# Loading the input tiles of a delta-rule attention kernel batch by batch

## The reference

```
x = x + layernorm(attention(layernorm(x)))
x = x + layernorm(ffn(layernorm(x)))
```

```
pred = wk @ S;  err = (v - pred) * beta;  S = S + outer(wk, err);  o = (rk @ S) * gate
```

## Time and profile before

| | us |
|---|---|
| median of 3 runs | 2324.56 |
| lowest, highest | 2321.91, 2326.44 |
| span of the profiled execution | 2313.7 |
| PE, DVE, ACT, POOL busy in it | 2084.1, 1992.1, 1774.0, 1729.0 |

### The profile page before, as it was taken

How to read it: one execution, slowest core, us unless ns; L and a number is a source line. 1 busy time by engine, 2 the same in 40 slices (tenths; PEclk the granted TensorE clock), 3 DMA queues, 4 the chain that set the end, 5 groups by cost and what they waited for, 6 DMA issues and landing times. The chain is left out here.

```text
span 2313.7 us, 123730 instructions
## 1 busy us (share of the span) xinstructions
PE 2084.1 (90%) x50216; PEld 1316.0 (57%) x50216; DVE 1992.1 (86%) x5810; ACT 1774.0 (77%) x3756; POOL 1729.0 (75%) x3099
## 2 busy tenths in 40 slices
PE   1679999999999999999999999999999987499997
PEld 1346666666666666666655656566666654255554
DVE  5388999999999999999889999899999994588886
ACT  3667888888888888888877878788888744477775
POOL 2668888888888888888888888888888854244443
PEclk7789999999999999999999999999999988799999
DMA  2122333333333333333333333333333222488885
GB/s 86 48 65 80 98 100 98 98 98 95 99 97 99 94 94 95 95 94 94 93 91 93 94 96 91 94 97 96 100 96 99 82 78 67 150 225 229 225 231 129
DMA packets 156632, 247.69 MB, mean 107 GB/s; under 512 B 39544, under 2 KB 39552, under 8 KB 156064
## 3 DMA queue, kind: packets, MB, share of 16 engines
q1 hardware_dynamic: 156064, 239.78, 36.6%
HBM read 104.40 MB, written 67.11 MB: 74 GB/s over the span
## 5 line engine op out<-in xcount | busy, mean ns | idle before, releaser
L800 DVE TENSOR_TENSOR ps_elim<-ps_elim,sys 128x30 f32<-128x30 f32 (+14 forms) x1920 | 543.3, 326 | 0.7
L808 DVE TENSOR_TENSOR sys<-sys,ps_elim 128x30 f32<-128x30 f32 (+14 forms) x1920 | 534.6, 316 | 1.0
L925 PE MATMUL ps_v<-wv,xt 128*128 128x512 f16 x1536 | 435.2, 389 | 39.6 <-DVE rhs L831 16.5
L925 PE MATMUL ps_y<-wo,ot 128*128 128x512 f16 x1536 | 406.1, 386 | 17.3 <-DVE x L852 9.5
L962 PEld LDWEIGHTS ps_chain<-rhs,t_t 32*32 32x32 f32 x16384 | 257.3, 144 | 110.6 <-issue 110.5
L962 PE MATMUL ps_chain<-rhs,t_t 32*32 32x32 f32 x16384 | 286.1, 218 | 13.9 <-issue 8.5
L709 ACT ACTIVATE state<-ps_s 128x512 f32<-128x512 f32 x128 | 76.5, 598 | 265.6 <-PE ps_s L1024 263.6
L1024 PEld LDWEIGHTS ps_s<-err,key_b 32*32 32x32 f32 x16384 | 172.1, 106 | 147.4 <-issue 147.2
L1310 PE MATMUL ps_f<-wq,f_xq 128*128 128x512 f16 x1024 | 242.5, 381 | 6.8 <-DVE f_xq L1276 6.8
L538 POOL TENSOR_TENSOR x_part<-x_hat,x_part 128x512 f16<-128x512 f32 x128 | 148.7, 1162 | 131.6 <-ACT x_hat L645 111.5
L1024 PE MATMUL ps_s<-err,key_b 32*32 32x32 f32 x16384 | 205.5, 195 | 34.2 <-issue 34.2
(11 more groups left out here) (163 smaller groups left out, 5123.6 us busy)
## 6 DMA issues: line engine op xcount, KB each, us to landing
x_in<-in_L_attn_x SPq DMA_DIRECT2D x128, 256.0 KB
kbd<-kt SPq DMA_DIRECT2D x512, 64.0 KB, 2.1
key_bd<-key_t SPq DMA_DIRECT2D x512, 64.0 KB, 2.4
x_res<-in_L_attn_x SPq DMA_DIRECT2D x128, 256.0 KB
x_scratch<-x SPq DMA_DIRECT2D x128, 256.0 KB, 6.3
f_x<-x_scratch SPq DMA_DIRECT2D x32, 1024.0 KB, 7.6
out<-f_res SPq DMA_DIRECT2D x128, 256.0 KB, 3.9
gate<-gates SPq DMA_DIRECT2D x128, 7.9 KB
```

Of the source, the lines that this page charges most:

```text
L800: dve.tensor_tensor(tmp, factors(r, c, first, end)[:, c - first:C - 1 - first, c - first:c - first + 1].to_broadcast(shape), sys[:, r, c:c ...
L808: dve.tensor_tensor(dst, dst, tmp, ALU.add).then_inc(elim_done[r], 1)
L925: last = pe.matmul(out, lhs[:, a, kb, :], weights[:, w, kb, :], start=(i == 0), stop=(i == 3 * KB - 1))
```

## The change

Each of the two loads is issued as four transfers, one per batch, of 32 rows of 2 KB each, in a loop. All four add to the same semaphore, so the waits count 64 per tile and not 16. Buffers, lags, order and all other work stay.

```diff
-                    sp.dma_start(tile(x_in, l % 4), rows(io["x"], base, j, LAG_LOAD)).then_inc(x_loaded[l % 4], 16)
+                    for b in range(B):
+                        sp.dma_start(x_in[C * b:C * b + C, l % 4, :], io["x"][b, C * n:C * n + C, :]).then_inc(x_loaded[l % 4], 16)
...
-                    sp.dma_start(tile(x_res, l % 2), rows(io["x"], base, j, LAG_Y)).then_inc(res_loaded[l % 2], 16)
+                    for b in range(B):
+                        sp.dma_start(x_res[C * b:C * b + C, l % 2, :], io["x"][b, C * n:C * n + C, :]).then_inc(res_loaded[l % 2], 16)
...
-                    act.wait_ge(x_loaded[l % 4], quads(base, j, LAG_STATS) * 16 + 16)
+                    act.wait_ge(x_loaded[l % 4], quads(base, j, LAG_STATS) * (16 * B) + 16 * B)
...
-                    act.wait_ge(x_loaded[l % 4], quads(base, j, LAG_XHAT) * 16 + 16)
+                    act.wait_ge(x_loaded[l % 4], quads(base, j, LAG_XHAT) * (16 * B) + 16 * B)
...
-                    dve.wait_ge(res_loaded[l % 2], halves(base, j, LAG_RES) * 16 + 16)
+                    dve.wait_ge(res_loaded[l % 2], halves(base, j, LAG_RES) * (16 * B) + 16 * B)
```

## The result

The changed kernel takes 2289.72 us (4 runs, 2287.3 to 2295.06) against 2325.5 us of the kernel before on the same chip: a ratio of 0.985 (95% interval 0.983 to 0.988), faster by 36 us. The forecast was faster by 11 us, 2313.5 us. The profile is of the slowest of the four runs (2295.06). One run in all that follows, the first of a repeat of the changed kernel, was in a slower state of the chip (granted clock 0.833 against 0.97, 2381.62 us) and is left out of its median.

The account below looks back on a forecast made before the run. SP's late issuing, beside the PE and DVE pair, was taken as the bound; with SP at 13.5 us a step, -6 - 3 - 1 - 4 + 3 = -11 us gave span 2302.7, plus 10.9 made 2313.5 us; full range 2297 to 2352.

Parts of the forecast that it names:

- What bounds the kernel: Attention part: PE and DVE tied as a pair, with SP, issuing all transfers, a bound beside them in two long stretches.
- Issues added: SP, each step: six more load issues at 0.48 us plus 0.04 gap, +3.12 us; the two that stay, -0.26.
- The jam: SP, at the four `key_bd` behind loads and gates: spread loads take off 4.1 us a step, leaving 0.6 for the gates.
- Collisions: SP's groups of issues: 0.9 more clashes a step with instruction queue packets at 0.77 us each, +0.7 us.
- Waits that go: Whole kernel: DVE's waits for `x_res` -6 us, PE's for `key_bd` -3 and for `kbd` -1.
- The start: Filling of the kernel: the first tiles' loads land sooner, so the third tile's statistics start earlier, -4 us.
- Costs elsewhere: PE's "issue" waits before `ps_s`: spread loads share engines with instruction fetch, +3 us, bounds 0 and 17.
- What lies around the span: Outside the profiled span: the runs' median lay 10.9 us above it, carried over unchanged to the forecast time.
- SP's relief is worth more: Rival, attention steps: 0.15 us per step comes back over 91 steps, 14 us more, 2299 us; chance 0.10.
- SP gets fuller: Rival: SP's step grows to 14.7 us, +55 us where SP is the bound, 2375; decided at 0.59 us pitch; chance 0.25.
- Quarters do not spread: Rival: 32-partition transfers run at a quarter rate, jam stays, some 113 steps grow about 2.9 us, 2650; chance 0.03.

Follow-up runs that it names:

- second profile: The kernel before, unchanged, profiled once more: 2324.01 us for a span of 2322.3.
- start-only kernel: Kernel before with only the `x_in` loads of the first four tiles split into four transfers: 2319.22 us, ratio 0.9985.
- only `x_in`: Kernel before with `x_in` split into four transfers and `x_res` left as one: 2301.43 us, ratio 0.990; repeated, 2300.86 us, ratio 0.989.
- gates in two parts: Kernel before with the gate transfer of 127 partitions cut into one of 112 and one of 15, loads single: 2302.65 us, ratio 0.990.
- the eighths: Changed kernel with both loads in eight transfers of 16 rows instead of four of 32: 2622.3 us, ratio 1.128 of the kernel before.

## Why the prediction was right in kind and wrong in size

*What bounds the kernel.* Right. SP was late in the long stretches, the jam made it so, and the edits that remove the jam, two of them without touching a load, gain 19 to 24 us.

*Issues added.* 0.48 us taken, 0.421 (`x_in`) and 0.425 (`x_res`) measured in the median, 0.310 at the least (the changed kernel's issues by line, ns min/median/max):

```profile
L431 SPq DMA_DIRECT2D x_in<-in_L_attn_x x512: 310/421/2059, 38.2 to 1757.4; - x171
...
L463 SPq DMA_DIRECT2D x_res<-in_L_attn_x x512: 310/425/1992, 185.5 to 1949.8; - x171
```

*The jam.* 0.6 us left for the gates, about 0.1 measured. *Collisions.* Right in kind. In the changed kernel's trace between 200 and 1750 us, the 76 groups of four `x_res` in whose first 2 us a packet of the instruction queue starts take 2.95 us in the mean, the other 32 take 2.06; for `kbd` it is 3.22 against 2.51, a difference near the 0.77 taken. Together SP's sum became 11.90 us, with about 0.04 of gap for each of 19 issues 12.7; I had 13.5. It matters little, as the time is flat below about 12 us of issue.

*Waits that go.* This is the step that failed. I took -6, -3 and -1 from one profile of the kernel before, as if its rows were the price. Two of them were low by chance: 7.3 us for `x_res` and 4.7 for `key_bd` there, 14.1 and 10.8 in the second profile, 12.8 and 12.1 in the profile of the start-only kernel, where steady work is the same. From the second profile, what went is -14.1 - 9.7 - 4.7 = -28.5 us where I had -10; even from the first it is -7.3 - 3.6 - 3.0 = -13.9. The second error is in the same place: I priced the waits one by one, while the runs show that what one of them is worth hangs on SP. Remove the `x_res` wait with SP late and nothing comes that could be told; in "only `x_in`", with SP early, it is 10.9 us.

*The start.* 4 taken, 3.5 measured alone (0.2 to 6.7), 4.4 between the two kernels of one chip that come nearest to differing in it. Beside other edits it isn't settled: with the gates in two parts it brings nothing (0.990 with and without it), with `x_res` in four as well about 10 us (2304.08 and 2293.45, on the same chip in two groups).

*Costs elsewhere.* +3 taken, nothing measured; the "issue" wait before `ps_s` went from 34.2 to 27.2 us.

*What lies around the span.* 10.9 us carried over from the median; in every run that has both it is 1.7 to 1.8 (2324.01 against 2322.3, 2295.06 against 2293.3). The profiled run of before was a quick one, with a span some 9 us under the usual. I took that distance for something fixed, while the second profile shows more waits of the kind that the change removes. So of the 23.8 us between forecast and result 9.1 are this carry-over; the other 14.7 lie between a span of 2302.7 and one of 2288.0, the usual one after the change.

Of the rivals, *SP's relief is worth more* (2299) was the closest, with 0.10, and still 9 us above the result. *SP gets fuller* is a real mechanism whose point of decision the eighths passed and the change did not. *Quarters do not spread* is false: `x_res` lands in 2.2 us. On "SBUF — State Buffer" of the Trainium skill ("Can I just issue two DMAs to hit both halves?"): four transfers of 64 KB land in 2.2 us each, and the store behind them in 2.2 where it took 6.3 behind the single one, so the case goes against reading it as a reason for one large transfer where that one has the 4 x 32 form. For a single transfer that itself runs on all engines no run here shows anything.

Left open: how the three terms add. `x_res` in four is worth 10.9 us on top of "only `x_in`" but nothing (+1.4, with intervals 13 and 14 us wide) on top of the gates in two parts, while that kernel with the start added as well reaches the changed one's time on two other occasions. The start, 3.5 us by itself, can't fill that gap. So 12 to 17 us of the 36 lie beyond the relief of SP, and of these only the start's 3.5 were measured alone. Also, the packets of the instruction queue go with the longer groups of issues, but why was not tested.

## What to carry to other kernels

Where one engine issues all transfers in program order, sum its issue times over one step and look at its own waits: near zero here meant that it was a bound, though no busy row showed it. Where the issue of a plain transfer takes far longer than its like, look at what was issued ahead of it: transfers that run on few engines, and behind them one whose number of partitions is awkward, as 127 was here and 128, or 112 and 15, were not. And take a profile of the kernel before twice, before any of its waits is used as a price.

## What the runs showed of the hardware

- The load of 4 x 32 rows moved on about four engines: a DMA share of 0.28 before, 99 GB/s at the start, and from before to after 60 more small packets per load (15,360 over 256 loads), as 4 to 64 completions would make. While four 32-row loads are issued the share is 0.55, though the rate in that 1 us is 98 GB/s as well. From issue to use the first tile took 3.3 us (38.17 to 41.45) and not 6.1 (38.4 to 44.54).
- The transfer of 127 partitions ended with 15 fewer small packets than that of 128, as one engine against 16 would; cut into 112 and 15 it had 30 more (3840 over 128 tiles).
- Behind two such loads and a transfer of 127 partitions the next issue took 5.0 us; with one row of 64 bytes more, over 128 partitions, 0.6 us, with the loads unchanged. That a small transfer decides whether a large one jams the issuing engine I had not expected.
- With 4.8 us of issues of loads in the place of 1.2 ahead of it, the jammed issue took 1.56 us and not 5.0, though these loads too ran on four engines each.
- Groups of four issues in whose first 2 us a packet of the instruction queue started were longer by 0.6 to 0.9 us (`x_res` 2.95 against 2.06, `kbd` 3.22 against 2.51, `key_bd` 3.27 against 2.67 in the changed kernel).
- The issue of a 32-row load from DRAM took 0.42 us in the median and 0.31 at the least, that of a 32-row transfer within SBUF 0.59.
- Executions of one program on one chip differ in how long PE and DVE wait for transfers: 12 against 25 us for `x_res` and `key_bd` together, at spans of 2313.7 and 2322.3.
